# The first norm of the coming group, applied by VectorE ahead of the score bands instead of by ScalarE among the head outputs

## The chip, the cores and the metric

The kernel runs on one core of a Trainium2 chip. The metric is the device time of one execution in microseconds. Its engines work side by side and meet at semaphores: TensorE (PE, matrix products into PSUM), VectorE (DVE), ScalarE (ACT), GpSimd (POOL) and SyncE (SP, which issues all DMAs here).

## The reference

One pre-norm decoder layer over 128 sequences of 128 tokens with 256 features, in float32:

```python
x = x + _L0_attn_ref(_layernorm(x), W_qkv, b_qkv, W_proj, b_proj)
x = x + _L0_xattn_ref(_layernorm(x), ctx_1024, ctx_1024, Wi_w, Wi_b, Wf_w, Wf_b, gn_w, gn_b)
x = x + _L0_ffn_ref(_layernorm(x), W1, b1, W2, b2, scale)
```

The first part is self-attention with one head, whose scaled scores are multiplied by a factor between 0.1 and 2 that depends on which of five bands of the sigmoid they fall into, before the softmax. The second is a gated cross-attention with eight heads, decays from cumulative sums of log sigmoids, and a norm over each head's output. The third is a feed-forward part of width 1024 with GELU and small per-sequence adapters. `_layernorm(x)` is `(x - mean) / sqrt(var + 1e-5)` over the features. The change concerns where the first of the three is applied to x.

## The kernel before

Four sequences (G = 4) form a group, so there are 32 groups, and tokens lie on the 128 partitions. The work is a software pipeline of steps, `it` from 0 to 33, written out by hand for each engine: steps 0 and 1 stand alone, steps 2 and on run in a hardware loop, the last ones stand alone again. In one step four groups are in flight: *coming* (group it+1, first norm, its transposes, projection to queries and values), *own* (group it, self-attention), *cross* (group it-1, cross-attention) and *ffn* (group it-2, feed-forward). The coming part runs in a prologue (`it` = -1) and in steps 0 to 30. Each engine executes its instructions in the written order, and every hand-over is a semaphore that counts up per step (`per_step`).

The first norm of the coming group takes this way. VectorE makes the statistics of `xin` (L858) and the variance (`ln_moments`, up to L871); ScalarE makes a first inverse root by Ln and Exp (L632, L633); VectorE improves it by one Newton step (`ln_scale`, L876 to L879) and makes `nmr` = -mean x rs (L1051). Later in the step ScalarE applies it: `apply_first` is four activations of 128x256, `xn1 = rs * xin + nmr` (L656). They stand between ScalarE's last decay exponential (L759) and its third head output (L772). TensorE then transposes `xn1` (`turn_xn1`, L1225) behind the last group of `pv` matmuls (L1508), ScalarE copies the result out twice (`xn1T` L648, `xn1h` L666), and TensorE projects (L1245 to L1262). The two other norms are applied by VectorE (`ln_apply`, L887).

What stands around the places of the change:

- VectorE, in order: the rows for the decays (L1044), `ln_scale` (L876 to L879), `nmr` (L1051), the score bands of the own group (L1055 to L1065), the row maximum (L1066, L1067, which signals `y_ok`), in step 0 alone the rest of the feed-forward weights (L1072) and the decay mask (L1075), then the transpose of the context (L1130), the weighing of the scores by the decays (L1101, two per sequence), the sums of the heads (L1111 to L1116), the sum with the residual (L1124), and the statistics of x2 (L858). L1169 closes the head sums.
- ScalarE, in order: feed-forward GELU (L750), an exponential (L791), the decay exponentials (`dexp`, L759, which L1101 waits for), the exponentials of the scores (`exps`, L780, which wait for `y_ok`), then the head outputs `hs` (L765), `ht` (L772, with the squares L775) with more `dexp` between them, and `apply_first` after the last `dexp`. After the fourth `ht` come the copies of `xn1T`, the wait for L1169 with L830 and L831, and `xn1h`.
- GpSimd: `xg` = x2 + bias (L612), which waits for `y_ok`; then four pieces of the head norm (L618), which wait for L1114 on VectorE. Earlier in the step, L595 to L605.
- SP: the context load waits for the last `pv` group (L505), and behind it the next x load (L482) waits for the applied first norm (L481).

The names in the profile are the tiles': `xn` stands for xn1, xn2 and xn3, `x` for x2, and the PSUM banks are UA, UB, TA, TB, DD, QQ, PV and GT.

Of the kernel before, what the change touches and what calls it, by code (L numbers as in the profile page):

```python
# [31 lines left out]
ALU = mybir.AluOpType  # L32
# [88 lines left out]
def build(nc, x, ctx_in, W_qkv, b_qkv, W_proj, b_proj, Wi_w, Wi_b, Wf_w, Wf_b, gn_w, gn_b,  # L121
# [4 lines left out]
    COMING = Stage(-1, NG - 2)  # L126
# [5 lines left out]
    with ctx:  # L132
        def sb(name, shape, dt=F32):
            return ctx.enter_context(nc.sbuf_tensor(name, shape, dt))

        def sem(name):
            return ctx.enter_context(nc.semaphore(name))
# [3 lines left out]
        def per_step(name, stage, per):  # L141

            c = Counter(sem(name), stage, per, 0 if stage is COMING else 1)
            if stage is not COMING:
                opened.append(c)
            return c

        def run(engine, step, chain=None, end=NG - 1):
# [15 lines left out]
        nmr = sb("nmr", [P, G])  # L164
# [29 lines left out]
        xin = sb("xin", [P, G, D])  # L194
        blocks = sb("blocks", [P, 2, N])
        xn1 = sb("xn1", [P, G, D])
# [68 lines left out]
        mean, half_gap, ve, lv, rs0, nt, rs = (  # L265
            sb(n, [P, 3, G]) for n in ("mean", "half_gap", "ve", "lv", "rs0", "nt", "rs"))
# [64 lines left out]
        xn1T_mm = per_step("xn1T_mm", COMING, 2)  # L331
# [46 lines left out]
        xn_ok = [per_step("xn1_ok", COMING, 1), per_step("xn2_ok", SELF, 1), per_step("xn3_ok", CROSS, 1)]  # L378
        rowterm_ok = per_step("rowterm_ok", SELF, 1)
        gate_ok = per_step("gate_ok", CROSS, 1)  # L380
        nmr_ok = per_step("nmr_ok", COMING, 1)
        z_ok = per_step("z_ok", FFN, 1)
        xn3l_ok = per_step("xn3l_ok", FFN, 2)
        t_ok = per_step("t_ok", FFN, 1)
# [241 lines left out]
        def _(act):  # L626
# [22 lines left out]

            def apply_first(it):  # L650

                act.wait_ge(nmr_ok.h, nmr_ok.at(it, 1))
                act.wait_ge(x_loaded.h, x_loaded.at(it, 16))
                act.wait_ge(xn1T_mm.h, xn1T_mm.at(it, 0))
                for b in range(G):
                    ins = act.activation(xn1[:, b, :], xin[:, b, :], ACT.Identity, bias=nmr[:, b:b + 1],  # L656
                                         scale=rs[:, 0, b:b + 1])
                ins.then_inc(xn_ok[0].h, 1)
# [24 lines left out]
            def evac_qT(it, m):  # L683
# [3 lines left out]
                act.activation(qT[:, m, :], TAB[m][:, :], ACT.Identity, bias=cq[:, m:m + 1]).then_inc(qT_ok.h, 1)  # L687

            apply_first(-1)
            evac_xn1T(-1, TAB)  # L690
            evac_xn1h(-1, TAB)
# [5 lines left out]
            def step(it):  # L697
# [58 lines left out]
                def dexp(b, hf):  # L756
                    act.wait_ge(d_mm.h, d_mm.at(it, 2 * b + hf + 1))
                    act.wait_ge(c_ok.h, c_ok.at(it, max(2 * b + hf - 1, 0)))
                    act.activation(dx[hf], DB[hf][:, :], ACT.Exp)\  # L759
                        .then_inc(dexp_ok.h, 1)  # L760
# [27 lines left out]
                cross, own, coming = CROSS.on(it), SELF.on(it), COMING.on(it)  # L788
# [21 lines left out]
                if cross:  # L810
                    dexp(3, 0)
                    hs(2)
                    dexp(3, 1)
                if coming:
                    apply_first(it)
                if isinstance(it, int) and it == 0:
                    for i in range(4):
                        act.wait_ge(raw_mm, 5 + i)
# [21 lines left out]
                if isinstance(it, int):  # L840
                    a.end()

            run(act, step, a)


        @block.vector
        def _(dve):
# [25 lines left out]
            def ln_scale(which, link):  # L873

                n, r0, e = nt[:, which, :], rs0[:, which, :], ve[:, which, :]
                link(dve.tensor_tensor(n, r0, r0, ALU.mult))  # L876
                link(dve.tensor_tensor(n, n, e, ALU.mult))
                link(dve.tensor_scalar(n, n, -0.5, 1.5, ALU.mult, ALU.add))
                link(dve.tensor_tensor(rs[:, which, :], n, r0, ALU.mult))  # L879

            def ln_apply(i, X, Xn):
                for b in range(G):
                    src, dst = X[:, b, :], Xn[:, b, :]
                    if i == 2:
                        src = src.rearrange("p (u c) -> p c u", c=CB)
                        dst = dst.rearrange("p (c u) -> p c u", c=CB)
                    ins = dve.tensor_scalar(dst, src, mean[:, i, b:b + 1], rs[:, i, b:b + 1], ALU.subtract, ALU.mult)  # L887
                ins.then_inc(xn_ok[i].h, 1)
# [5 lines left out]
            dve.wait_ge(rs0_ok.h, 1)  # L894
            ln_scale(0, done)
            dve.scalar_tensor_tensor(nmr[:, :], mean[:, 0, :], -1.0, rs[:, 0, :], ALU.mult, ALU.mult)\
               .then_inc(nmr_ok.h, 1)

            def xn1_low(it):
                dve.wait_ge(up_mm.h, up_mm.at(it, KH))  # L900
# [72 lines left out]
            def step(it):  # L973
                coming, own, cross, ffn = COMING.on(it), SELF.on(it), CROSS.on(it), FFN.on(it)
# [73 lines left out]
                if coming:  # L1048
                    dve.wait_ge(rs0_ok.h, rs0_ok.at(it, 1))
                    ln_scale(0, link)  # L1050
                    dve.scalar_tensor_tensor(nmr[:, :], mean[:, 0, :], -1.0, rs[:, 0, :], ALU.mult, ALU.mult)\  # L1051
                       .then_inc(nmr_ok.h, 1)
                if own:
                    dve.wait_ge(sc_ok.h, sc_ok.at(it, 1))
                    band_lo = v.mark(dve.tensor_scalar(band_a[:, :], sc[:, :], BANDS[0], 0.3, ALU.is_ge, ALU.mult))  # L1055
# [155 lines left out]
                if isinstance(it, int):  # L1211
                    v.end()

            run(dve, step, v)


# [416 lines left out]
```

## Time and profile before

| what | value |
|---|---|
| median of 3 runs | 1842.91 us (1842.37 to 1843.39) |
| profiled execution | 1841.88 us |
| its span, first to last instruction | 1840.2 us |
| mean granted TensorE clock | 0.983 |
| TensorE busy | 1765.3 us, 96% |
| VectorE busy | 1338.2 us, 73% |
| ScalarE busy | 1153.0 us, 63% |
| GpSimd busy | 318.1 us, 17% |

The busy shares are averages over the whole span. The table of stretches and the order of instructions in one step tell more about a change that moves work inside a step; the first two steps, in which the pipeline fills, have to be read by themselves. All rows are from the profiled execution.

### The profile page before, as it was taken

The numbers are of one execution on the slowest core, as the hardware profiler recorded it, in microseconds if no ns is written. First come the engines' busy times: TensorE is split into PE (matmuls) and PEld (weight loads), VectorE is DVE, ScalarE is ACT, GpSimd is POOL, SyncE is SP. The second block draws the span as 40 slices with busy tenths as digits, with TensorE's granted clock in tenths as the row PEclk, the third lists the DMA queues.
The fourth block names the chain that finished last, engine by engine and source line by source line (L and its number), as shares of the span: only waits on it lengthen the run. The fifth ranks groups of instructions, "written<-read, shape, count | busy, mean of one in ns | idle before, by whom it ended". The sixth has DMA issues, their size and how long they took to land.

```text
span 1840.2 us, 44267 instructions
## 1 busy us (share of the span) xinstructions
PE 1765.3 (96%) x14172; PEld 1370.0 (74%) x14172; DVE 1338.2 (73%) x3901; ACT 1153.0 (63%) x2634; POOL 318.1 (17%) x301
## 2 busy tenths in 40 slices
PE   5669999999999999999999999999999999999897
PEld 4557777877777777777778777777877777777675
DVE  4677777777777777777777777777777777777752
ACT  1456766666676666677666667766666676666552
POOL 2012211111221112122111212211111211111110
PEclk8879999999999999999999999999999999999998
DMA  5111212221121222112122211212221212221100
GB/s 136 35 38 37 60 37 60 60 59 48 36 60 37 60 60 59 41 43 60 37 60 60 59 35 49 55 43 60 60 57 29 58 45 52 60 60 39 24 15 26
DMA packets 222639, 92.35 MB, mean 50 GB/s; under 512 B 150785, under 2 KB 222082, under 8 KB 222610
## 3 DMA queue, kind: packets, MB, share of 16 engines
q1 hardware_dynamic: 222610, 91.99, 19.0%
q8 instruction: 15, 0.25, 0.1%
q14 instruction: 14, 0.11, 0.0%
HBM read 70.71 MB, written 16.78 MB: 48 GB/s over the span
## 4 chain that ended last, share of the span: by engine, by line
PE 93%; DVE 4%; ACT 1%; issue 1%; DMA 0%; SPq 0%; DVEq 0%; ACTq 0%
PE UA L1462 11%; PE TA L1462 6%; PE UB L1400 6%; PE GT L1462 5%; PE TB L1400 5%; PE PV L1400 5%; PE UA L1425 3%; PE GT L1473 3%; PE TA L1362 3%; PE QQ L1225 3%; PE TA L1400 3%; PE UA L1400 3%; PE DD L1225 2%; PE PV L1508 2%; PE QQ L1493 2%; PE UB L1508 2%
## 5 line engine op out<-in xcount | busy, mean ns | idle before, releaser
L1101 DVE TENSOR_TENSOR C<-qT,QKs 128x512 f32<-128x512 f32 x256 | 178.5, 718 | 173.0 <-ACT qT L759 170.1
L1462 PE MATMUL UA<-W2f,hs_all 128*128 128x256 f32 x1024 | 231.5, 379 | 0.0
L1462 PEld LDWEIGHTS UA<-W2f,hs_all 128*128 128x128 f32 x1024 | 194.4, 190 | 30.5 <-issue 0.2
L618 POOL TENSOR_TENSOR Ng<-HT,gnw_b 128x256 f32<-128x256 f32 x128 | 93.4, 729 | 497.5 <-DVE cden L1114 492.9
L595 POOL TENSOR_TENSOR vc<-vc 128x992 f32<-128x992 f32 x32 | 59.0, 1843 | 632.8 <-DVE ve L871 631.8
L612 POOL TENSOR_TENSOR xg<-x,gnb_b 128x1024 f32<-128x1024 f32 x32 | 75.6, 2362 | 300.7 <-DVE nmx L1067 284.3
L1462 PE MATMUL TA<-W2f,hs_all 128*128 128x256 f32 x512 | 120.8, 379 | 0.0
L1462 PE MATMUL GT<-W2f,hs_all 128*128 128x256 f32 x512 | 115.7, 379 | 0.0
L672 ACT ACTIVATE V<-QQ 128x260 f32<-128x260 f32 x32 | 12.4, 388 | 159.4 <-PE QQ L1257 159.4
L1462 PEld LDWEIGHTS GT<-W2f,hs_all 128*128 128x128 f32 x512 | 94.9, 190 | 11.6
L1462 PEld LDWEIGHTS TA<-W2f,hs_all 128*128 128x128 f32 x512 | 94.9, 190 | 11.3
L740 ACT ACTIVATE QKs<-DD 128x512 f32<-128x512 f32 x64 | 38.4, 599 | 89.6 <-PE DD L1425 89.6
L704 ACT ACTIVATE xn3T<-QQ 128x512 f32<-128x512 f32 x32 | 19.1, 597 | 105.9 <-PE QQ L1225 105.9
L1425 PEld LDWEIGHTS UA<-xn2T,ctxT 32*128 32x128 f32 x512 | 63.2, 190 | 26.7 <-issue 12.9
L605 POOL TENSOR_TENSOR xb<-xb,cvp 128x1024 f32<-128x1024 f32 x32 | 76.1, 2378 | 30.2 <-DMA xb<-x 17.6
L1425 PE MATMUL UA<-xn2T,ctxT 32*128 32x128 f32 x512 | 75.6, 287 | 3.5 <-ACT QKs L740 2.2
L1225 PE MATMUL QQ<-ident,xn 128*128 128x128 f32 x380 | 62.4, 288 | 15.0 <-DVE xn L887 13.6
L1023 DVE COPY acs<-DD 32x128 f32<-32x128 f32 x32 | 9.0, 282 | 92.8 <-PE DD L1358 92.8
L1425 PE MATMUL QQ<-xn2T,ctxT 32*128 32x128 f32 x512 | 75.7, 288 | 0.0
L1425 PE MATMUL GT<-xn2T,ctxT 32*128 32x128 f32 x512 | 75.7, 288 | 0.0
L1425 PE MATMUL DD<-xn2T,ctxT 32*128 32x128 f32 x512 | 75.6, 288 | 0.0
L759 ACT ACTIVATE qT<-DD 128x512 f32<-128x512 f32 x128 | 74.0, 578 | 2.5 <-DVE C L1101 1.4
(385 smaller groups left out, 5286.3 us busy)
## 6 DMA issues: line engine op xcount, KB each, us to landing
xin<-x SPq DMA_DIRECT2D x32, 512.0 KB, 4.4
xb<-x SPq DMA_DIRECT2D x32, 512.0 KB, 4.1
blocks<-ctx SPq DMA_DIRECT2D x256, 64.0 KB, 2.0
vc<-ctx SPq DMA_DIRECT2D x32, 512.0 KB, 3.6
out<-ot SPq DMA_DIRECT2D x32, 512.0 KB, 3.2
Ev<-xn SPq DMA_DIRECT2D x512, 1.0 KB
hs_all<-L_ffn_W SPq DMA_DIRECT2D x4, 512.0 KB, 8.9
E<-xn SPq DMA_DIRECT2D x128, 16.0 KB
```

Of the source, the lines that this page charges most:

```text
L595: pool.tensor_tensor(heads[:, :, 0:HD - 1], heads[:, :, 0:HD - 1], heads[:, :, HD - 1:HD].broadcast_to([P, G * HEADS, HD - 1]), ALU.subtra ...
L605: pool.tensor_tensor(xb[:, :, :], xb[:, :, :], cvp[:, :].unsqueeze(1).broadcast_to([P, G, D]), ALU.add).then_inc(xb_ok.h, 1)
L612: pool.tensor_tensor(xg[:, :, :], x2[:, :, :], gnb_b[:, :].unsqueeze(1).broadcast_to([P, G, D]), ALU.add).then_inc(xg_ok.h, 1)
L618: pool.tensor_tensor(Ng[:, b, :].rearrange("p (k n) -> p k n", k=2), HT[:, b % 2, :, 0:P], gnw_b[:, :].rearrange("p (k n) -> p k n", k=2), ...
L759: act.activation(dx[hf], DB[hf][:, :], ACT.Exp)\
L1101: dve.tensor_tensor(C[:, b % 2, :, half], dx[hf].rearrange("p (h i) -> p h i", h=HEADS), QKs[:, b, :, half], ALU.mult)\
L1225: ins = pe.transpose(banks[c][:, b * S:(b + 1) * S], src[:, b, c * P:(c + 1) * P], ident[:, :])
L1362: ins = pe.matmul(TAB[0][:, b * S:(b + 1) * S], qT[:, k, b * S:(b + 1) * S], xn1T[:, k, b * S:(b + 1) * S], start=(k == 0), stop=(k == 1))
L1400: pe.matmul(UP[i][:, :], w[:, k, hc * P:(hc + 1) * P], xt[:, k, :], start=(w is W1h and xt is xn3h and k == 0), stop=False)
L1425: ins = pe.matmul(QKB[r][:, (2 * b + f) * P:(2 * b + f + 1) * P], ctxT[lane, f, tok], xn2T[lane, f, tok], start=True, stop=True)
L1462: ins = pe.matmul(OB[b][:, 0:D], hs_all[:, k, b * S:(b + 1) * S], W2f[:, k, :], start=(i == 0), stop=(i == KH - 1))
L1508: ins = pe.matmul(bank[q:q + 32, (h // 4) * P:(h // 4 + 1) * P], vc[:, b, HD * h:HD * h + HD], C[:, b % 2, h, :], start=True, stop=True)
```

## The change

VectorE applies the first norm of the coming group right after it has made the factor `rs`, before the score bands, by the function it uses for the other two norms: four `tensor_scalar` instructions, `(xin - mean) * rs`, 128x256 each. They signal `xn1_ok`, which ScalarE's apply signalled before. `nmr` is no longer made in the steps, and ScalarE's `apply_first` is left in the prologue alone (`it` = -1), with a plain semaphore. VectorE gets the wait for TensorE's transposes of the step before (`xn1T_mm`), which protects `xn1` from being overwritten and stood on ScalarE before.

```diff
-        nmr_ok = per_step("nmr_ok", COMING, 1)
+        nmr_ok = sem("first_nmr")
...
             def apply_first(it):
 
-                act.wait_ge(nmr_ok.h, nmr_ok.at(it, 1))
+                act.wait_ge(nmr_ok, 1)
...
                     dexp(3, 0)
                     hs(2)
                     dexp(3, 1)
-                if coming:
-                    apply_first(it)
...
             dve.scalar_tensor_tensor(nmr[:, :], mean[:, 0, :], -1.0, rs[:, 0, :], ALU.mult, ALU.mult)\
-               .then_inc(nmr_ok.h, 1)
+               .then_inc(nmr_ok, 1)
...
                 if coming:
                     dve.wait_ge(rs0_ok.h, rs0_ok.at(it, 1))
                     ln_scale(0, link)
-                    dve.scalar_tensor_tensor(nmr[:, :], mean[:, 0, :], -1.0, rs[:, 0, :], ALU.mult, ALU.mult)\
-                       .then_inc(nmr_ok.h, 1)
+                    dve.wait_ge(xn1T_mm.h, xn1T_mm.at(it, 0))
+                    ln_apply(0, xin, xn1)
                 if own:
                     dve.wait_ge(sc_ok.h, sc_ok.at(it, 1))
```

## Rows read from the trace of the kernel before

**Rows 1.** The page: part 1 (busy time and share) and part 4 (chain).

```profile
PE 1765.3 (96%) x14172; PEld 1370.0 (74%) x14172; DVE 1338.2 (73%) x3901; ACT 1153.0 (63%) x2634; POOL 318.1 (17%) x301
...
PE 93%; DVE 4%; ACT 1%; issue 1%; DMA 0%; SPq 0%; DVEq 0%; ACTq 0%
```

**Rows 2.** Stretches: length, then busy us by engine, granted clock, DMA share, GB/s.

```profile
60.00:120.00 60.00, 34.78 (x313) 28.04 (x314) 40.85 (x111) 28.45 (x73) 9.82 (x8) 0.76 0.14 36
...
900.00:1000.00 100.00, 99.94 (x812) 78.00 (x811) 77.19 (x226) 65.36 (x152) 15.10 (x14) 1.00 0.18 50
```

**Rows 3.** Timeline, VectorE, 900 to 910: start us, us, line, out<-in, [idle before].

```profile
901.11 0.16 DVE L1051 SCALAR_TENSOR_TENSOR nmr<-mean,rs 128x4 f32<-128x4 f32 x1
901.18 0.42 DVE L1055 TENSOR_SCALAR bands<-sc 128x512 f32<-128x512 f32 x1
...
905.55 1.25 DVE L1130 STREAM_TRANSPOSE ctxT<-blocks 128x1024 f32<-128x1024 f32 x1
909.75 1.29 DVE L1101 TENSOR_TENSOR C<-qT,QKs 128x512 f32<-128x512 f32 x2 [2.96 <-ACT qT L759]
```

**Rows 4.** Timeline, VectorE, the two norms already applied there, 935 to 939.

```profile
935.72 1.77 DVE L887 TENSOR_SCALAR xn<-xg,mean,rs 128x256 f32<-128x256 f32 x4
937.41 1.37 DVE L887 TENSOR_SCALAR xn<-x,mean,rs 128x256 f32<-128x256 f32 x4
938.70 0.41 DVE L1084 TENSOR_TENSOR ot<-GT,ot 128x256 f32<-128x256 f32 x1
```

**Rows 5.** Single lines: count, ns shortest/median/longest, first and last start.

```profile
L656 ACT ACTIVATE xn<-xin,nmr,rs x128: 584/590/610, 8.3 to 1675.1; 128x256 f32<-128x256 f32 x128
...
L887 DVE TENSOR_SCALAR xn<-x,mean,rs x128: 401/407/415, 78.5 to 1746.9; 128x256 f32<-128x256 f32 x128
...
L1051 DVE SCALAR_TENSOR_TENSOR nmr<-mean,rs x31: 161/164/165, 46.7 to 1655.2; 128x4 f32<-128x4 f32 x31
```

**Rows 6.** Timeline, ScalarE, 919 to 927.

```profile
919.51 2.06 ACT L656 ACTIVATE xn<-xin,nmr,rs 128x256 f32<-128x256 f32 x4
921.48 0.37 ACT L772 ACTIVATE HT<-PV 128x264 f32<-128x264 f32 x1
...
926.72 0.23 ACT L830 ACTIVATE htmp<-harg 128x32 f32<-128x32 f32 x1 [0.38 <-DVE harg L1169]
```

**Rows 7.** Timeline, TensorE, the same step.

```profile
911.10 0.65 PE L1508 MATMUL PV<-C,vc 128*32 128x128 f32 x16
...
919.68 0.61 PE L1515 MATMUL PV<-centre,HS 128*128 128x132 f32 x4
...
922.95 0.66 PE L1225 MATMUL QQ<-ident,xn 128*128 128x128 f32 x4
```

**Rows 8.** Waits, 300 to 1600 us: who on whom, total us, times, longest.

```profile
PEld QQ L1245 <- ACT xn3h L666: 6.1, 24, 0.3
```

**Rows 9.** Timeline, GpSimd: step 1, then the steady step.

```profile
97.28 2.35 POOL L612 TENSOR_TENSOR xg<-x,gnb_b 128x1024 f32<-128x1024 f32 x1 [8.22 <-DVE nmx L1067]
...
905.77 2.36 POOL L612 TENSOR_TENSOR xg<-x,gnb_b 128x1024 f32<-128x1024 f32 x1 [9.16 <-DVE nmx L1067]
```

**Rows 10.** Timeline, VectorE, steps 0 and 1.

```profile
47.42 0.43 DVE L1055 TENSOR_SCALAR bands<-sc 128x512 f32<-128x512 f32 x1 [0.54 <-ACT sc L724]
...
92.79 0.16 DVE L1051 SCALAR_TENSOR_TENSOR nmr<-mean,rs 128x4 f32<-128x4 f32 x1
...
98.28 1.90 DVE L1101 TENSOR_TENSOR C<-qT,QKs 128x512 f32<-128x512 f32 x1
```

**Rows 11.** Chain that ended last, step 0: start us, us, what.

```profile
57.77 2.30 DVE moving L1075
```

**Rows 12.** Timeline, TensorE, steps 0 and 1.

```profile
63.25 1.99 PE L1333 MATMUL UA<-ident,hs_all 128*64 128x128 f32 x16 [4.38 <-DVE x L1124]
...
100.88 1.08 PE L1508 MATMUL PV<-C,vc 128*32 128x128 f32 x16 [3.83 <-issue]
...
117.49 0.56 PE L1245 MATMUL QQ<-Wvh,xn3h 128*128 128x260 f32 x2 [4.29 <-ACT xn3h L666]
```

## The prediction, made before the change was run

> **What bounds the kernel now.** I read the page first. Part 1 has TensorE busy for 96% of the span, VectorE for 73% and ScalarE for 63%, and the chain that ended last is 93% TensorE [rows 1]. The stretches say where that holds: between 900 and 1000 us TensorE is busy 99.94 of 100 us at full clock, between 60 and 120 us only 34.78 of 60, at a granted clock of 0.76 [rows 2]. So there are two regimes. In the steady steps, one every 53.87 us (L1051 at 901.11 and, 14 steps on, at 1655.2 [rows 3, 5]), TensorE is the bound, and a change on another engine counts only where it makes TensorE wait or ends such a wait. In steps 0 and 1 little is in flight and the chain runs through VectorE and ScalarE too. The two are worked out apart.
>
> **What goes and what comes.** ScalarE loses L656, four instructions of 590 ns in each step with a coming group; four together take 2.06 us [rows 5, 6]. 128 are counted, four of them before step 0; so 31 steps lose 2.06 us each, 64 us of busy time. VectorE loses L1051 (31 x 164 ns = 5 us) and gains four L887 in each of the 31 steps. Their form is that of the L887 already there from x2 (SBUF to SBUF, contiguous, two scalars per partition): 407 ns each [rows 5], and what stands behind four of them starts 1.29 us after the first (937.41 to 938.70) [rows 4]. L1051 holds its successor back by only 0.07 us (901.11 to 901.18) [rows 3]. So the score bands begin 1.29 - 0.07 = 1.22 us later wherever VectorE is not itself waiting. The form of L887 that reads in strides holds the next one back by 1.69 us (935.72 to 937.41) [rows 4]; that is the upper bound, a delay of 1.62 us. The new source is contiguous, so I take 1.22, and for the lower bound as well, since nothing here reads less. The added wait, for the transposes of the step before, was satisfied some 30 us earlier (they start at 922.95 [rows 7], the next L1051 at 901.11 + 53.87 = 954.98). Its price is an issue slot: not below nothing, and at most the 0.07 us by which L1051 holds back its successor. I take 0.
>
> **Steady steps, VectorE's side.** Queued behind the four new instructions are the bands (L1055 to L1067), the transpose of the context (L1130) and the first weighing, L1101. L1130 starts at 906.77 instead of 905.55. L1101 starts at 909.75 after idling 2.96 us for ScalarE's exponential [rows 3], so 2.96 - 1.22 = 1.74 us of cover are left. Who waits for the bands: ScalarE's exponentials of the scores, which stand in ScalarE's order behind the very exponentials for which L1101 waits until 909.75, three microseconds after the bands' new end; and GpSimd's L612, at 905.77 now, which moves to 906.99 and ends at 909.35 [rows 9]. The pieces of L618 behind it need TensorE's and ScalarE's later head work. TensorE's first matmul on the result of L1101 starts at 911.10 [rows 7] and does not move. Price: 0.
>
> **Steady steps, ScalarE's side.** The 2.06 us at 919.51 go. Behind them stands L772 at 921.48 [rows 6], whose input TensorE made from 919.68 to 920.29 [rows 7], so it can start about 1.1 us earlier. After it ScalarE waits for TensorE's own order again, and the reader of L772 on VectorE, L1111, stands behind the norm statistics of x2. TensorE's transposes of the applied norm start at 922.95 [rows 7], and the apply ended at 919.51 + 2.06 = 921.57: it was 1.4 us in time already. The time saved on ScalarE was not on the path; what is late next is unchanged. Gain: 0. On the SP queue the next x load waits for the apply, but stands behind the context load, which waits for the last L1508 group; that group ends when the transposes at 922.95 are due, after the old apply's end. So this load stays where it is, and in step 0 (where that wait is open from the start) it comes early into an idle queue.
>
> **Steps 0 and 1.** In step 0 L1051 starts at 46.7 [rows 5] and the bands at 47.42, after 0.54 us of waiting for ScalarE's scores [rows 10]. Four applies put the bands at 46.7 + 1.29 = 48.0, that is 0.6 us later. From there VectorE is the chain: its last piece of L1075 starts at 57.77 and takes 2.30 us [rows 11], then come L1130 and L1124, and at 63.25 TensorE is let go after 4.38 us of idling for L1124 [rows 12]. So 0.6 us are paid. ScalarE's copies behind its old apply come earlier, but what they let go ends in that same wait. In step 1 L1051 stands at 92.79 and VectorE runs on through the bands and L1130 into L1101 at 98.28, with no idle time shown before it [rows 10]; TensorE sits idle for 3.83 us until 100.88 [rows 12], when the second L1101 is done. So 1.22 us are paid. TensorE's turning of the coming norm can come earlier in step 1, but behind it TensorE idles for 4.29 us until 117.49 [rows 12] for copies that stand behind VectorE's L1169, so that is worth nothing. Step 2 onward is bound by TensorE and keeps the shift. Sum: 0.6 + 1.2 + 29 x 0 = 1.8 us.
>
> **Contention with GpSimd, weighed.** In step 1 L1101 starts at 98.28 inside L612 (97.28 to 99.63) [rows 9] and takes 1.90 us [rows 10]; in the steady step the two instructions from 909.75 take 1.29 us together [rows 3]. In step 1 both are late by 1.22 us, so that overlap stays. In the steady step L612 will end at 909.35, 0.40 us before L1101 starts. The Trainium skill, "GPSIMD Engine Reference", Key points, says that GpSimd shares its SBUF interfaces with VectorE and that VectorE instructions with two SBUF inputs contend for them; the rows of step 1 agree. By this rule the change is free only while L612 ends ahead of L1101. As a mechanism of this kernel it is the first rival.
>
> **Rivals.** (1) Slower: the bands come later than reckoned, L612 runs into L1101, and TensorE waits in every step. It decides from a delay of 1.22 + 0.40 = 1.62 us, just the bound by the strided form. L1101 has 0.1 us to spare before L1508 (909.75 + 1.29 = 911.04 against 911.10 [rows 3, 7]), so each 0.1 us beyond costs about 29 x 0.1 = 2.9 us; 0.3 us beyond gives 1.8 + 8.7 = 10.5, or 1853.4. For it speak the thin margins, against it how constant the form is (401 to 415 ns [rows 5]). (2) Faster: ScalarE's relief reaches TensorE. The only place that the waits show is ScalarE's copy that starts the projection, for which the weight loads of L1245 idled 6.1 us in 24 steps, 0.25 us each [rows 8]. If all of it went, 29 x 0.25 = 7.3 us against 1.8 us: 1837.4. Against it: that copy stands behind ScalarE's wait for VectorE's L1169 (L830 idles 0.38 us for it at 926.72 [rows 6]), which the apply does not touch. (3) The start pays another amount. TensorE's idle stretch in step 0 grows, and the granted clock is 0.76 there [rows 2]. If it is back from 1.2 to 2.4 GHz 2 us later in each of the two steps, half of that is lost, 2 x 1 = 2 us: 1846.7. If the chain of the two steps has slack that I don't see, nothing is paid: 1842.9. (4) The change doesn't do what it says: the applied norm would have to be late for TensorE, and it is ready some 19 us earlier than before (902.5 against 921.57); nothing speaks for it.
>
> **How the numbers follow.** The profiled execution took 1841.88 us with a span of 1840.2; the median of the runs is 1842.91 (1842.37 to 1843.39), 1.0 above it. The sum puts the span at 1842.0, the profiled execution at 1843.7 and the median at 1844.7. About 0.2% (3.7 us) is what a measurement of this kernel can tell from no change, so 1839.2 to 1846.6 is the same. Forecast: 0.68. Rival 3: 0.16, nearly all of it inside 0.2%. Rival 1: 0.09, two parts in three beyond 0.2%. Rival 2: 0.06. Rival 4: 0.01. The range takes in the forecast with the spread of the runs, rival 3, and the mild part of rival 1: 1841.5 to 1848. Faster 0.05, same 0.86, slower 0.09.
>
> **What would show it.** Four more L887 of about 0.41 us behind L879; the idle time of L1101 before the exponential down from 2.96 to about 1.7 us; L612 ending before L1101 starts; the third L772 about 1.1 us earlier in the step; the step still 53.87 us and TensorE busy 99.94 of 100; the first steady step begun some 1.8 us later. A step of over 54.0 us, or an L1101 above 0.8 us right behind L612, would prove the forecast wrong; so would a start that is no later.

## The result

The changed kernel takes 1844.99 us (median of 20 runs, 1843.64 to 1847.16) against 1842.64 us for the kernel before (20 runs, 1840.26 to 1843.43): a ratio of 1.0016, with a 95% interval of 1.001 to 1.0023. It is about 2.4 us slower by the medians and 2.9 us by the ratio, inside the 0.2% set as the bound. The forecast was 1844.7, a cost of 1.8 us. The profiled execution has a span of 1843.6 us instead of 1840.2, at a mean granted clock of 0.981 instead of 0.983. Two executions among those of the experiments, of 7257 and 4745 us, lie far outside all others and are left out of the ratios below.

The page of the kernel after, parts 1 and 4, and two stretches of it (columns as in [rows 2]):

```profile
PE 1766.9 (96%) x14172; PEld 1372.1 (74%) x14172; DVE 1374.3 (75%) x3994; ACT 1095.4 (59%) x2510; POOL 318.1 (17%) x301
...
PE 93%; DVE 4%; ACT 1%; issue 1%; DMA 0%; SPq 0%; DVEq 0%; ACTq 0%
...
60.00:120.00 60.00, 32.49 (x302) 25.91 (x303) 40.58 (x111) 26.83 (x69) 9.82 (x8) 0.76 0.14 36
...
900.00:1000.00 100.00, 99.95 (x812) 78.14 (x811) 80.00 (x231) 61.92 (x143) 14.97 (x13) 1.00 0.16 45
```

Beside [rows 1, 2]: ScalarE lost 57.6 us of busy time, VectorE gained 36.1, and the chain is divided as before. The middle of the kernel is as full as before (99.95 of 100 us). Between 60 and 120 us TensorE did 2.3 us less work than before in the same time. Most of the loss is there; about 1 us of it comes just behind.

**The steady step after.** VectorE's timeline, then GpSimd's and ScalarE's in the same step, then three rows of waits between 300 and 1600 us:

```profile
903.76 0.16 DVE L877 TENSOR_TENSOR rs<-nt,rs 128x4 f32<-128x4 f32 x1
904.05 1.38 DVE L885 TENSOR_SCALAR xn<-xin,mean,rs 128x256 f32<-128x256 f32 x4
905.35 0.42 DVE L1053 TENSOR_SCALAR bands<-sc 128x512 f32<-128x512 f32 x1
...
912.67 1.29 DVE L1099 TENSOR_TENSOR C<-qT,QKs 128x512 f32<-128x512 f32 x2 [1.72 <-ACT qT L759]
...
909.93 2.36 POOL L612 TENSOR_TENSOR xg<-x,gnb_b 128x1024 f32<-128x1024 f32 x1 [10.36 <-DVE nmx L1065]
...
923.25 0.39 ACT L772 ACTIVATE HT<-PV 128x264 f32<-128x264 f32 x1 [0.72 <-PE PV L1513]
...
DVE C L1099 <- ACT qT L759: 95.9, 96, 1.7
PEld PV L1506 <- DVE C L1099: 7.7, 24, 0.3
PEld QQ L1243 <- ACT xn3h L666: 6.2, 24, 0.3
```

The four applies stand in 904.05 to 905.35 and hold the bands back by 1.30 us. The idle time before the weighing (now L1099) went from 2.96 us [rows 3] to 1.72. L612 ends at 909.93 + 2.36 = 912.29, which is 0.38 us before the weighing starts. The third L772 comes 10.58 us after the start of the weighing instead of 11.73 [rows 3, 6], 1.15 us earlier, and now waits for TensorE. The wait of the projection's weights (now L1243) is 6.2 us where it was 6.1 [rows 8]. The step can be measured by one matmul group in two places of TensorE's timeline, 13 steps apart (`GT<-xn3T,Z`, the first matmuls of a step's feed-forward part):

```profile
943.58 0.65 PE L1379 MATMUL GT<-xn3T,Z 128*32 128x128 f32 x16
...
1643.54 0.64 PE L1379 MATMUL GT<-xn3T,Z 128*32 128x128 f32 x16
```

(1643.54 - 943.58) / 13 = 53.84 us. By the same group the kernel before has (1640.91 - 940.65) / 13 = 53.87.

**Steps 0 and 1 after.** VectorE's timeline, then TensorE's:

```profile
46.98 1.39 DVE L885 TENSOR_SCALAR xn<-xin,mean,rs 128x256 f32<-128x256 f32 x4
48.27 0.43 DVE L1053 TENSOR_SCALAR bands<-sc 128x512 f32<-128x512 f32 x1
...
93.71 1.38 DVE L885 TENSOR_SCALAR xn<-xin,mean,rs 128x256 f32<-128x256 f32 x4
95.01 0.42 DVE L1053 TENSOR_SCALAR bands<-sc 128x512 f32<-128x512 f32 x1
...
100.42 3.31 DVE L1099 TENSOR_TENSOR C<-qT,QKs 128x512 f32<-128x512 f32 x3
...
64.08 1.99 PE L1331 MATMUL UA<-ident,hs_all 128*64 128x128 f32 x16 [5.51 <-DVE x L1122]
...
103.02 1.08 PE L1506 MATMUL PV<-C,vc 128*32 128x128 f32 x16 [5.05 <-issue]
...
106.94 1.08 PE L1506 MATMUL UB<-C,vc 128*32 128x128 f32 x16
...
119.80 0.80 PE L1243 MATMUL QQ<-Wvh,xn3h 128*128 128x260 f32 x2 [5.02 <-ACT xn3h L666]
...
123.44 1.05 PE L1250 MATMUL TA<-xn3h,Awh 128*128 128x512 f32 x2
...
131.54 0.80 PE L1223 MATMUL QQ<-ident,xn 128*128 128x128 f32 x4 [3.43 <-DVE xn L885]
...
132.99 3.06 PE L1360 MATMUL TA<-xn1T,qT 128*128 128x128 f32 x16
...
135.98 0.64 PE L1379 MATMUL GT<-xn3T,Z 128*32 128x128 f32 x16
```

Four rows of the kernel before, same view, that answer to the later ones:

```profile
104.51 0.65 PE L1508 MATMUL UB<-C,vc 128*32 128x128 f32 x16
...
120.88 0.79 PE L1252 MATMUL TA<-xn3h,Awh 128*128 128x512 f32 x2
...
128.39 1.11 PE L1225 MATMUL QQ<-ident,xn 128*128 128x128 f32 x4 [3.43 <-DVE xn L887]
...
132.66 0.65 PE L1381 MATMUL GT<-xn3T,Z 128*32 128x128 f32 x16
```

I take as the *stretch* the time from the instruction that follows the last one of `rs` in step 0 (before: L1051 at 46.72; after: L885 at 46.98) to the `GT<-xn3T,Z` group of step 2. It is 132.66 - 46.72 = 85.94 us before and 135.98 - 46.98 = 89.00 after: 3.06 us more, of the 3.4 by which the spans differ. Its pieces are:

| from, to | before | after | difference |
|---|---|---|---|
| step 0's slot to step 1's (92.79; 93.71) | 46.07 | 46.73 | +0.66 |
| to the first `pv` group of step 1 (100.88; 103.02) | 8.09 | 9.31 | +1.22 |
| to the projection (117.49; 119.80) | 16.61 | 16.78 | +0.17 |
| to the transposes for step 2 (128.39; 131.54) | 10.90 | 11.74 | +0.84 |
| to the `GT` group of step 2 (132.66; 135.98) | 4.27 | 4.44 | +0.17 |

The first two pieces, 1.88 us, are the two terms of the forecast (0.6 and 1.2). The other three, 1.18 us, were not in its sum. In them the same matmuls are shorter or longer: the second `pv` group takes 1.08 us instead of 0.65, the first L1250 group 1.05 instead of 0.79. The granted clock over the first `pv` group is 0.50 in both kernels; over the second it is 1.00 before (104.51 to 105.16) and 0.50 after (106.94 to 108.02). So 1.08 us is this group at 1.2 GHz and 0.65 the same group at 2.4. From the start of the projection to the start of its last group TensorE works without a pause, for 6.85 us before (117.49 to 124.34) and 7.68 after (119.80 to 127.48): 0.83 of the 0.84 us of the fourth piece. Stretches of the kernel before, then of the kernel after:

```profile
100.00:110.00 10.00, 8.55 (x78) 6.30 (x78) 6.43 (x16) 6.69 (x16) 1.46 (x2) 0.79 0.01 2
...
120.00:130.00 10.00, 6.57 (x33) 5.68 (x33) 6.91 (x24) 3.08 (x9) 0.00 (x0) 0.84 0.01 3
```

```profile
100.00:110.00 10.00, 6.87 (x53) 4.77 (x53) 6.54 (x11) 5.44 (x16) 2.50 (x2) 0.60 0.01 2
...
120.00:130.00 10.00, 8.11 (x36) 7.04 (x36) 6.61 (x21) 2.71 (x8) 0.00 (x0) 0.75 0.00 0
```

The granted clock after is 0.60 instead of 0.79 and 0.75 instead of 0.84. These stretches lie at the same times and not at the same work, which comes 2 to 3 us later in the kernel after. Over the 10 us that begin with the first `pv` group it is 0.75 (from 103.02) instead of 0.84 (from 100.88), over those that begin with the projection 0.74 (from 119.80) instead of 0.83 (from 117.49). Ahead of the `pv` group TensorE idled for 5.05 us instead of 3.83 [rows 12], ahead of the projection for 5.02 instead of 4.29: in step 1 its transposes no longer wait for ScalarE's apply (0.48 us before, at 111.49), so it is done earlier and idles longer for the same copy.

### The profile page after: what moved, and what is told of

The parts are those of the page before. It is cut to its first block, busy times and chain, and to the rows that moved or that the text cites. A ratio compares the mean times of both kernels' runs of the same rounds, so it can differ in the third digit from the quotient of the medians.

```text
span 1843.6 us, 44178 instructions
## 1 busy us (share of the span) xinstructions
PE 1766.9 (96%) x14172; PEld 1372.1 (74%) x14172; DVE 1374.3 (75%) x3994; ACT 1095.4 (59%) x2510; POOL 318.1 (17%) x301
## 3 DMA queue, kind: packets, MB, share of 16 engines
HBM read 70.71 MB, written 16.78 MB: 47 GB/s over the span
## 4 chain that ended last, share of the span: by engine, by line
PE 93%; DVE 4%; ACT 1%; issue 1%; DMA 0%; SPq 0%; DVEq 0%; ACTq 0%
PE UA L1460 11%; PE TA L1460 6%; PE UB L1398 6%; PE GT L1460 5%; PE TB L1398 5%; PE PV L1398 5%; PE UA L1423 3%; PE GT L1471 3%; PE TA L1360 3%; PE QQ L1223 3%; PE TA L1398 3%; PE UA L1398 3%; PE DD L1223 2%; PE PV L1506 2%; PE QQ L1491 2%; PE UB L1506 2%
## 5 line engine op out<-in xcount | busy, mean ns | idle before, releaser
L1099 DVE TENSOR_TENSOR C<-qT,QKs 128x512 f32<-128x512 f32 x256 | 178.5, 718 | 137.4 <-ACT qT L759 134.5
L612 POOL TENSOR_TENSOR xg<-x,gnb_b 128x1024 f32<-128x1024 f32 x32 | 75.6, 2363 | 336.4 <-DVE nmx L1065 320.0
L759 ACT ACTIVATE qT<-QQ 128x512 f32<-128x512 f32 x128 | 75.1, 587 | 0.1
```

Of the source, the lines that this page charges most:

```text
L612: pool.tensor_tensor(xg[:, :, :], x2[:, :, :], gnb_b[:, :].unsqueeze(1).broadcast_to([P, G, D]), ALU.add).then_inc(xg_ok.h, 1)
L1099: dve.tensor_tensor(C[:, b % 2, :, half], dx[hf].rearrange("p (h i) -> p h i", h=HEADS), QKs[:, b, :, half], ALU.mult)\
```

## The experiments

**Where the cost is: the steady steps or the first two.** The theory puts all of it into steps 0 and 1; the rival lets the steady steps pay by contention. Two kernels split the change. In `loop_only` ScalarE still applies the norm in steps 0 and 1, and VectorE from step 2 on:

```diff
...
+                if isinstance(it, int) and it in (0, 1):
+                    apply_first(it)
...
-                    dve.wait_ge(xn1T_mm.h, xn1T_mm.at(it, 0))
-                    ln_apply(0, xin, xn1)
+                    if isinstance(it, int) and it in (0, 1):
+                        dve.scalar_tensor_tensor(nmr[:, :], mean[:, 0, :], -1.0, rs[:, 0, :], ALU.mult, ALU.mult)\
+                           .then_inc(nmr_ok, 1)
+                    else:
+                        dve.wait_ge(xn1T_mm.h, xn1T_mm.at(it, 0))
+                        ln_apply(0, xin, xn1)
```

> VectorE applies the norm in the steps from 2 on; in steps 0 and 1 ScalarE does it as before. Theory (the cost lies in steps 0 and 1 alone, steady steps are free): as fast as the kernel before, ratio 1.000 within 0.0007, first steady step begun at the same time, step 53.87 us. Rival (each steady step pays some 0.1 us that the trace of before hides): ratio 1.0012 to 1.002, step 53.95 us or more.

`start_only` is the reverse: the kernel before, with VectorE applying in steps 0 and 1.

> VectorE applies the norm in steps 0 and 1 alone; in the later steps ScalarE does it as before. Theory: the whole cost of the change, 2 to 3.5 us, ratio 1.0011 to 1.0019, of which 0.6 us in step 0, 1.2 us in step 1 and the rest as matmuls at 1.2 GHz for longer. Rival (steady steps pay): within 1 us of the kernel before.

Measured: `loop_only` 1842.41 us, ratio 1.0002 (0.9993 to 1.0011), stretch 86.08 us, step 53.87. `start_only` 1845.85 us, ratio 1.0020 (1.0011 to 1.0029), stretch 89.17, step 53.86. The whole cost is made by the two first steps, and the other 29 cost nothing that can be seen: the interval of `loop_only` ends at 1.0011, 0.07 us a step, and its step is that of the kernel before. The busy time that ScalarE is spared in them bought nothing either.

**Which of the two.** The kernel after, with ScalarE's apply kept in one step alone: the same edit with `it in (1,)` or `it in (0,)`.

> The change, but ScalarE applies the norm in step 1 as before; VectorE does in step 0 and from step 2 on. Theory (step 0 costs 0.6 us, step 1 1.2 us): from the factor rs of step 0 to the first matmuls of step 2's feed-forward part (gram) some 86.5 us (before 85.9, after 89.0), time 0.3 to 1.5 us over the kernel before, ratio 1.0002 to 1.0008. Rival (the whole cost comes from step 0, whose longer idle time lets TensorE's clock return later): as slow as after, 89 us and ratio 1.0013 or more.

> The change, but ScalarE applies the norm in step 0 as before; VectorE does from step 1 on. Theory: 87.2 us over the same stretch if the clock returns as in before, 88.3 if it returns late as in after; ratio 1.0007 to 1.0013. Rival (step 0 carries the cost): 85.9 us and ratio 1.000.

Measured: with ScalarE in step 1, 1843.25 us, ratio 1.0007 (0.9998 to 1.0017), stretch 86.45: only step 0's share, 0.5 us, is left. With ScalarE in step 0, 1844.93 us, ratio 1.0014 (1.0005 to 1.0024), stretch 88.95: as long as that of the whole change, and above both numbers expected. So the terms don't simply add. In the first kernel TensorE's second `pv` group takes 0.64 us, in the second 1.08: the late clock comes with the change of step 1. In the second kernel step 0's piece is back at 46.17 us (44.92 to 91.09), 0.56 less than after, but the pieces behind the first `pv` group take 33.47 us instead of 32.96 after and 31.78 before. What step 0 gave back was lost again to the clock, which costs 1.69 us here and 1.18 in the kernel after.

That the late return belongs to the change of step 1 doesn't rest on one pair of executions. The three traces in which VectorE applies in step 1 (`after`, `start_only`, `scalar_in_step0`) have the second `pv` group at 1.08 us and stretches of 88.95 to 89.17. The five in which ScalarE does (before, `loop_only`, `scalar_in_step1` and the two fillers below) have it at 0.64 or 0.65 and stretches of 85.94 to 86.45.

**The clock by itself.** If the 1.18 us behind 103.02 are the clock's, then work for TensorE in its 5 us gap should take them away. `warm_after` is the kernel after with 20 transposes of a weight into PSUM bank TB, which nobody uses then, ahead of the first `pv` of step 1; their results are read by nobody.

```diff
+                    if isinstance(it, int) and it == 1:
+                        for i in range(20):
+                            pe.transpose(TAB[1][:, (i % 4) * S:(i % 4 + 1) * S], W2f[:, i % 8, 0:P], ident[:, :])
```

> The change, with 20 idle 128x128 transposes of a weight on TensorE in step 1, in its 5.05 us of idling before the first weighted values (L1506 of after, L1508 of before); at most 4.3 us at 1.2 GHz, so they hold nothing up, and their results are not used. Theory (beyond the 1.8 us that VectorE's queue costs, the change costs over 1 us because the longer idling lets TensorE's clock return later): the clock is back before the second group of those matmuls (0.65 us instead of 1.08), the stretch from the factor rs of step 0 to gram of step 2 falls from 89.0 to 87.8 us or less, the ratio from 1.0016 to 1.0010 or less. Rival (the clock's return is no part of it): stretch 89.0, ratio 1.0016.

Measured: 1841.71 us, ratio 0.9999 (0.999 to 1.0008), stretch 86.27. TensorE's timeline of `warm_after`, and one stretch:

```profile
98.19 4.05 PE L1552 MATMUL TB<-ident,W2f 128*128 128x128 f32 x20
...
103.47 0.64 PE L1506 MATMUL PV<-C,vc 128*32 128x128 f32 x16 [1.23 <-issue]
...
105.89 0.64 PE L1506 MATMUL UB<-C,vc 128*32 128x128 f32 x16 [0.24 <-ACT HT L772]
...
118.56 0.67 PE L1243 MATMUL QQ<-Wvh,xn3h 128*128 128x260 f32 x2 [5.00 <-ACT xn3h L666]
...
100.00:110.00 10.00, 8.27 (x85) 6.22 (x84) 7.92 (x16) 7.00 (x22) 3.54 (x3) 0.92 0.01 2
```

The first `pv` group starts as late behind the slot as in the kernel after (103.47 - 47.38 = 56.09 us, against 103.02 - 46.98 = 56.04), so the queue's 1.88 us are still paid. But both groups take 0.64 us, at a granted clock of 0.92, and the projection comes 15.09 us behind the first group instead of 16.78. The stretch loses 2.73 us, more than the 1.18 that I gave to the clock: in the kernel before, too, the first `pv` group runs at 1.2 GHz [rows 12], and this kernel gains that as well. So the run shows that a late clock costs microseconds here and that work in the gap ends it. It does not by itself say how much of the change's cost is the clock's; the table of pieces does. It also clears the second gap: ahead of the projection TensorE idled for 5.00 us here, as long as in the kernel after, and the piece behind it is 10.90 us, as in the kernel before.

**Contention behind a thin margin.** The first rival's mechanism needs the bands later by more than the margin. `filler_ahead` is `loop_only` with an instruction of 1.24 us whose result nobody reads, between the apply and the bands; `filler_behind` has it behind the row maximum, so that VectorE has the same work while L612 starts when it did.

```diff
+                        dve.transpose(spare[:, :, :].rearrange("p a b -> p (a b)"),
+                                      W2f[:, 0:4, :].rearrange("p a b -> p (a b)"))
```

> Built on the kernel of loop_only. From step 2 on VectorE also does one idle transpose of 1024 elements (about 1.2 us, its result is not used) behind the applied norm and ahead of the score bands, so that the bands, GpSimd's bias addition (L612) and the first weighing's turn on VectorE all come 1.2 us later still. VectorE's own cover before the first weighing (1.66 us in loop_only) is enough, the distance between L612's end and the first weighing (0.31 us) is not. Theory (the two contend): L612 runs about 0.9 us into the first weighing, which takes 1.5 us or more instead of 0.69; the step grows by 0.6 to 0.9 us, the time by 18 to 27 us, ratio 1.010 to 1.015. Rival (only the order of the queue counts): ratio within 0.001 of 1.

> As filler_ahead, but the idle transpose stands behind the row maximum that releases GpSimd's L612, and ahead of the context transpose. VectorE's queue before the first weighing is as long as in filler_ahead, only L612 isn't later. Theory: the first weighing is not lengthened, its idle time before falls from 1.66 to about 0.45 us, the step stays 53.87 us, ratio within 0.001 of 1. Rival (it is VectorE's queue that is full): as slow as filler_ahead.

Measured: `filler_ahead` 1863.71 us, ratio 1.0117 (1.01 to 1.0133). `filler_behind` 1842.06 us, ratio 0.9999 (0.9989 to 1.0009). The steady step of `filler_ahead` (VectorE, GpSimd, TensorE, and a row of its waits):

```profile
913.34 1.24 DVE L1058 STREAM_TRANSPOSE spare<-W2f 128x1024 f32<-128x1024 f32 x1
...
920.57 2.01 DVE L1108 TENSOR_TENSOR C<-qT,QKs 128x512 f32<-128x512 f32 x2 [0.50 <-ACT qT L760]
...
919.05 2.37 POOL L613 TENSOR_TENSOR xg<-x,gnb_b 128x1024 f32<-128x1024 f32 x1 [11.58 <-DVE nmx L1074]
...
922.63 0.64 PE L1515 MATMUL PV<-C,vc 128*32 128x128 f32 x16 [0.73 <-DVE C L1108]
...
PE PV L1515 <- DVE C L1108: 17.7, 24, 0.7
```

and that of `filler_behind`:

```profile
907.83 1.24 DVE L1074 STREAM_TRANSPOSE spare<-W2f 128x1024 f32<-128x1024 f32 x1
...
910.84 1.29 DVE L1109 TENSOR_TENSOR C<-qT,QKs 128x512 f32<-128x512 f32 x2 [0.64 <-ACT qT L760]
...
908.17 2.37 POOL L613 TENSOR_TENSOR xg<-x,gnb_b 128x1024 f32<-128x1024 f32 x1 [10.46 <-DVE nmx L1072]
```

With the filler ahead, GpSimd works until 921.42, the weighing starts at 920.57, and its two instructions take 2.01 us instead of 1.29. TensorE waits 0.7 us for them in each of the 24 steps looked at. The spans differ by 1861.6 - 1841.4 = 20.2 us, 0.70 us in each of 29 steps. With the filler behind, GpSimd ends at 910.54, 0.30 us ahead of the weighing, and nothing is lost although VectorE has the same work. So the rival's mechanism is real, and its price is what the prediction said: the bands are late by 1.32 + 1.16 = 2.48 us against the order of the kernel before, 0.78 us beyond the point of decision (1.32 + 0.38), and at 0.1 us of spare ahead of TensorE that gives 0.68 x 29 = 20 us. The change itself did not reach that point.

**A version that is faster than both.** The chain of step 0 ran through the two instructions of the decay mask (L1075, [rows 11]), which need nothing from this step. `before_mask` is the kernel before with them at the start of step 0, where VectorE idles; `loop_mask` and `after_mask` do the same to `loop_only` and to the kernel after, and `warm_mask` adds 14 idle transposes to `before_mask`.

```diff
... at the start of VectorE's step
+                if isinstance(it, int) and it == 0:
+                    for t in range(2):
+                        heads = slice(2 * HEADS * t, 2 * HEADS * (t + 1))
+                        link(dve.tensor_tensor(moving[:, heads, :].rearrange("p h (f i) -> p h f i", f=2),
...
... behind the row maximum
-                    for t in range(2):
-                        heads = slice(2 * HEADS * t, 2 * HEADS * (t + 1))
-                        link(dve.tensor_tensor(moving[:, heads, :].rearrange("p h (f i) -> p h f i", f=2),
...
```

> The kernel before, with the two instructions that make the decay mask (4.6 us on VectorE in step 0, ahead of the residual sums) moved to the start of step 0, where VectorE idles for 7.5 us. Theory (VectorE's queue is the chain of step 0): the residual sums come 4.6 us earlier and the time falls by 3 to 5 us, ratio 0.9973 to 0.9984; the 0.6 us of the change would then be paid by the same queue. Rival (step 0 is held by something else, and the cost of the change there is only seen shifted): less than 1 us gained.

> Both: VectorE applies the norm from step 2 on, ScalarE in steps 0 and 1, and the decay mask is made at the start of step 0. Theory: the same as the kernel before with the mask moved, 3 to 5 us less than before; it beats both kernels, by the mask and not by the norm. Rival (steady steps pay): 2 us slower than the kernel before with the mask moved.

> The change together with the decay mask made early. In step 0 TensorE then waits for ScalarE's copy of a weight (0.93 us in before_mask), which stands behind ScalarE's apply, and the change takes that apply away; so VectorE's 0.6 us may be met by ScalarE's relief. Theory: step 0 free or nearly so, step 1 still 1.2 us and a late clock, so 1 to 3 us over the mask alone: ratio 0.9973 to 0.9983 against the kernel before. Rival (step 1 is free as well): 0.9967.

> The kernel before with the decay mask made early, and with 14 such idle transposes in step 1's idle time of 3.83 us (at most 3.0 us at 1.2 GHz). Theory: 1 to 2 us less than the mask alone, ratio 0.9955 to 0.9963 against the kernel before. Rival: as the mask alone, 0.9967.

| kernel | median us | ratio (95%) | stretch us |
|---|---|---|---|
| before_mask | 1836.34 | 0.9967 (0.9956 to 0.9978) | 79.77 |
| warm_mask | 1835.97 | 0.9963 (0.9949 to 0.9976) | 79.12 |
| loop_mask | 1837.85 | 0.9973 (0.9962 to 0.9984) | 81.75 |
| after_mask | 1839.69 | 0.9987 (0.9978 to 0.9996) | 84.87 |

The mask's move is worth 6 us, more than I gave it. TensorE no longer idles ahead of the group that turns `hs_all`, and that group runs at 2.4 GHz (granted clock 1.00 from 57.18 to 59.30, against 0.50 over the same group before): this is TensorE's row of `before_mask` for the group that takes 1.99 us at 63.25 in the kernel before [rows 12].

```profile
57.18 1.23 PE L1334 MATMUL UA<-ident,hs_all 128*64 128x128 f32 x16
```

The change of the norm costs its share with the mask early, too. By the traces `after_mask` is 5.1 us of stretch above `before_mask`; by the medians it is 3.35 us, against 2.4 without the mask's move, so that it costs more than without is not shown. Its ratio, 0.9987, lies a little above the 0.9973 to 0.9983 expected (its interval takes them in), and step 0 was not free as expected: its piece is 41.92 us (46.15 to 88.07) against 40.20 (45.09 to 85.29). TensorE waits for the exponentials of the scores at 53.52, behind VectorE's bands, for 1.93 us instead of 1.34, and then runs at a granted clock of 0.71 until its turns of `hs_all` at 59.33, where it had 1.00 in `before_mask`.

Three things don't fit a rule by which the length of the idling decides. `loop_mask` has the same work in steps 0 and 1 as `before_mask`, in the same order, and its stretch is 2 us longer, with the second `pv` group of step 1 at 1.2 GHz after idling for only 3.82 us. `after_mask` idles for 3.06 us there and has the same late clock. And the idle transposes of `warm_mask` were to gain 1 to 2 us and can't be told from none by the medians: its trace gains 1.33 us between the first `pv` group and the projection (15.09 us for 16.42), and loses 0.81 behind it, with the first L1253 group at 1.05 us instead of 0.63, although TensorE idled for 4.29 us ahead of the projection in one and 4.28 in the other. So how long TensorE idles before it does not alone decide when the clock returns; what else does stays open.

## Why the prediction was right, and where it was not

- **Steady steps cost nothing: right, and shown.** Step 53.84 against 53.87, `loop_only` at 1.0002. The steps of the working hold: four applies of 407 ns (404 to 415 in the trace after), 0.38 us between L612 and the weighing where 0.40 was reckoned, the third L772 earlier by 1.15 us for 1.1, no gain from it.
- **The bands' delay: right, a little small.** In the loop VectorE's bands start 1.59 us behind the start of the last `rs` instruction instead of 0.27, so the delay is 1.32 us, not 1.22. The term that was too small is the added wait: in the loop the first apply starts 0.29 us behind L877, where L1051 stood 0.20 behind L879, 0.09 us more against a bound of 0.07; in steps 0 and 1, where it is a wait on a constant, the distance is 0.20 (93.51 to 93.71), so nothing. That the 0.09 us are the wait's is argued: no run takes the wait away alone. It cost no time: the weighing moved with ScalarE's exponential, and 0.38 us between L612 and the weighing were left. In step 2 of `loop_only` L612 ended 0.05 us before the weighing (156.29 and 156.34), still without cost.
- **Step 0, 0.6 us: right.** The bands come 0.85 us later (47.42 to 48.27), of which 0.27 us is an earlier offset between the two executions: 0.58. TensorE idles 5.51 us instead of 4.38 ahead of the turns [rows 12], but step 1 begins only 0.66 us later.
- **Step 1, 1.2 us: right in the queue, short on what follows it.** The weighing comes 2.14 us later (98.28 to 100.42), 0.92 of which step 1 inherits, so 1.22 is its own. Its first three instructions take 3.31 us in both traces: the overlap with L612 stayed, as said. What was missing in the sum is the clock. The prediction had it as a price of rival 3, up to 1 us in each of the two steps, and took 0 for the forecast. It measured 1.18 us in the pieces, all of it from step 1 on and none in step 0, so the stretch grew by 3.06 us instead of 1.8. Nothing in the trace of before said 0: TensorE stood at 1.2 GHz after the very gap that the change lengthens [rows 12], so the value nearer to the row was not 0.
- **Rival 1 (contention): its mechanism shown, its condition not met.** The pair of fillers has it with 20 us.
- **Rival 2 (ScalarE's relief): fell.** The wait on L666 is 6.2 us after 6.1, as the order of ScalarE's copies behind VectorE's L1169 said. ScalarE lost 57.6 us of busy time where 64 was reckoned: the four activations overlap by about 0.1 us with the instruction on either side (919.01 + 0.60 against 919.51, 921.57 against 921.48), so a step is spared some 1.87 us.
- **Rival 4 (no effect): fell.** The apply is done by VectorE at 904.05.
- **The move of the x load: as said.** In step 0 it is issued at 48.39 instead of 56.78, into an idle queue, and nobody gains.

The end of the kernel is not explained to the tenth. The shift against the kernel before is 3.3 us at step 2, 2.6 us at step 30 (1643.54 against 1640.91) and 3.4 us at the end of the span. The 0.7 us regained on the way are the 53.84 us a step against 53.87; `loop_only`, with the same loop, doesn't have them. The last steps varied by up to 1.2 us between kernels with the same work there (from that group to the end 200.06 us in `after`, 198.88 in `after_mask`). And the start of the stretch lies between 44.92 and 47.67 us in the traces of all kernels, which have the same work ahead of it but for the mask. The median of 20 runs, 2.4 us, is therefore not told apart from either sum, 1.8 or 3.1, and that the forecast of 1844.7 lies 0.3 us from the median is in part luck; `start_only` and `scalar_in_step1` say that the difference to the kernel before is real and is made in step 1 for the most part.

## What to carry to other kernels

Here TensorE was the bound, and work moved from ScalarE to VectorE, which both had slack, cost nothing in the steady steps and gained nothing, since ScalarE was not on the path; the price was paid where the pipeline fills and VectorE's queue is the chain. So cost the fill apart from the steady steps. In it, add to the delay of the queue what TensorE may lose by running at 1.2 GHz for longer (1.2 to 1.7 us here), and look for work in that queue which the step does not need, since moving that was worth more than the change. Where a transfer of work leaves a few tenths of a microsecond between GpSimd's instruction and VectorE's next one with two inputs, write that margin down: beyond it each step paid, 0.70 us for an instruction of 1.24 us put in the wrong place.

## What was not expected of the hardware

- Twenty transposes with no reader in a gap of TensorE's, 4.05 us of work, shortened the stretch behind them by 2.73 us.
- VectorE's transpose of the context took 1.25 us beside L612, about as long as the 1.24 of the filler's transpose with GpSimd idle, while the weighing, which reads two operands, took 2.01 us for two instructions instead of 1.29.
- Behind the added wait VectorE started 0.09 us later in the looped steps and no later in the steps outside of the loop.
- With 3.82 us of idling ahead of them the same matmuls got their clock back early in `before_mask` (3.83 us) and late in `loop_mask`.
